# A feed-forward block in which GpSimd rounds the tokens and adds the outputs, and VectorE takes the statistics at the end of its turn

## The reference

```python
def bitlinear(x, W, b):
    w_scale = jnp.clip(jnp.mean(jnp.abs(W)), EPS, None)
    Wq = _ste(W, jnp.clip(jnp.round(W / w_scale), -1.0, 1.0) * w_scale)
    x_scale = jnp.clip(jnp.max(jnp.abs(x), axis=-1, keepdims=True), EPS, None)
    xq = _ste(x, jnp.clip(jnp.round(x * (QB / x_scale)), -QB - 1.0, QB) * (x_scale / QB))
    return jnp.einsum('bnd,hd->bnh', xq, Wq) + b
h = bitlinear(x, W1, b1)
h = jax.nn.gelu(h, approximate=False)
return bitlinear(h, W2, b2)
...
x = x + _L0_ffn_ref(_layernorm(x, axis=-1), L0_ffn_W1, L0_ffn_b1, L0_ffn_W2, L0_ffn_b2)
```

## Time and profile before

| | us |
|---|---|
| median of 3 runs | 934.14 (934.08 to 935.68) |
| span of the profiled execution, first to last instruction | 930.7 |
| own time of the profiled execution | not listed apart; the median lies 3.4 over the span |
| busy in the span: PE, DVE, ACT, POOL | 870.6, 631.0, 532.4, 388.8 |
| stretch 53.35 to 142.48, feed-forward turns: DVE, ACT, PE, POOL busy of 89.13 | 77.15, 68.14, 68.11, 41.87 |

### The profile page before, as it was taken

How to read it: one execution, slowest core, us unless ns; L and a number is a source line. 1 busy time by engine, 2 the same in 40 slices (tenths; PEclk the granted TensorE clock), 3 DMA queues, 4 the chain that set the end, 5 groups by cost and what they waited for, 6 DMA issues and landing times.

```text
span 930.7 us, 14992 instructions
## 1 busy us (share of the span) xinstructions
PE 870.6 (94%) x4295; PEld 611.3 (66%) x4300; DVE 631.0 (68%) x1274; ACT 532.4 (57%) x851; POOL 388.8 (42%) x334
## 2 busy tenths in 40 slices
PE   9977789889999999999999999999999999999992
PEld 4635455544555545555467787878888888888881
DVE  5788987856557557456388779856666666666666
ACT  2558885455675665765555534326666666666650
POOL 2144455434775746656505645612222222222210
PEclk9999999999999999999999999999999999999996
DMA  9500000019469578568564200078711288526405
GB/s 305 113 1 1 0 1 1 1 43 367 176 232 352 183 288 335 195 281 315 227 249 173 121 1 1 13 287 368 280 63 34 65 339 339 223 81 260 110 17 181
DMA packets 49909, 154.07 MB, mean 166 GB/s; under 512 B 6266, under 2 KB 24438, under 8 KB 44236
## 3 DMA queue, kind: packets, MB, share of 16 engines
q1 hardware_dynamic: 46124, 144.25, 41.3%
q0 software_dynamic: 3744, 9.31, 3.2%
HBM read 97.85 MB, written 56.62 MB: 166 GB/s over the span
## 4 chain that ended last, share of the span: by engine, by line
PE 68%; DVE 16%; ACT 6%; issue 4%; DMA 2%; POOL 2%; SPq 1%; DVEq 0%; ACTq 0%; POOLq 0%
PE banks L1043 12%; PE banks L1294 8%; PE banks L1296 8%; PE banks L1295 8%; PE banks L1012 4%; PE banks L1035 3%; PE banks L1036 3%; PE banks L1331 2%; PE banks L1333 2%; PE banks L1332 2%; PE banks L1307 2%; PE banks L950 2%; PE banks L916 1%; PE banks L999 1%; PE banks L1057 1%
## 5 line engine op out<-in xcount | busy, mean ns | idle before, releaser
L1043 PE MATMUL banks<-wexp 128*65 128x512 f32 (+1 forms) x288 | 148.1, 595 | 3.3 <-ACT wexp L1608 3.3
L674 POOL TENSOR_TENSOR cv_hl<-wexp,cv_hl 128x1024 fp32r<-128x1024 f32 x45 | 108.5, 2419 | 55.0 <-ACT cv_hl L1585 54.4
L1294 PE MATMUL banks<-ring,x_hi 128*128 x312 | 127.4, 408 | 0.0
L1296 PE MATMUL banks<-ring,x_lo 128*128 x312 | 122.1, 391 | 0.0
L1295 PE MATMUL banks<-ring,x_hi 128*128 x312 | 122.0, 391 | 0.0
L1608 ACT ACTIVATE wexp<-banks 128x512 f32<-128x512 f32 x128 | 76.5, 600 | 69.2 <-PE banks L1036 68.8
L2097 DVE TENSOR_REDUCE small<-banks 128x1 bf16<-128x1101 f32 x64 | 83.7, 1307 | 38.5 <-PE banks L1012 38.5
L1744 ACT ACTIVATE banks<-wexp 128x1024 f32 x72 | 73.5, 1020 | 47.7 <-DVE aux L2488 47.7
L1722 ACT ACTIVATE aux<-banks 128x512 f32<-128x512 f32 x78 | 46.7, 598 | 61.2 <-PE banks L1296 45.2
L1035 PE MATMUL banks<-q_hi,k_hl 128*128 128x512 f32 x144 | 74.3, 516 | 1.7 <-ACT q_lo L1576 1.0
L1296 PEld LDWEIGHTS banks<-ring,x_lo 128*128 128x128 f32 x312 | 58.6, 188 | 13.1
(11 more groups left out here) (373 smaller groups left out, 2186.6 us busy)
## 6 DMA issues: line engine op xcount, KB each, us to landing
wsplit<-cv_hl SPq DMA_DIRECT2D x45, 1024.0 KB, 8.0
ring<-wsplit SPq DMA_DIRECT2D x32, 1280.0 KB
wexp<-in_L_ffn_w SPq DMA_DIRECT2D x40, 512.0 KB, 5.9
wexp<-in_expert_biases SPq DMA_DIRECT2D x8, 1152.0 KB, 6.5
ring<-wsplit SPq DMA_DIRECT2D x4, 1024.0 KB, 8.3
wexp<-moe_y SPq DMA_DIRECT2D x7, 512.0 KB, 5.9
wexp<-in_L_ffn_sw SPq DMA_DIRECT2D x5, 512.0 KB, 10.2
x_sb<-in_x SPq DMA_DIRECT2D x4, 512.0 KB, 7.8
```

Source lines behind the costliest of these rows:

```text
L674: g.tensor_tensor(sides(hl[:, PIECE:2 * PIECE]), raw, sides(hl[:, 0:PIECE]).bitcast(f32), ALU.subtract).then_inc(s['cv_lo'], 1)
L1043: mm(pb[5 + half][0:DA, :], vh[b][0:w, c, :], pT[q % 3][0:w, :], start=c == 0, stop=c == len(KTILES) - 1).then_inc(s['a_pv'], 1)
L1294: mm(o[:], x_hi[u][:, kc, :], hi, start=kc == 0 and not primed, stop=False, skip_group_check=primed)
L1296: last = mm(o[:], x_lo[u][:, kc, :], hi, start=False, stop=primed and kc == KC - 1, skip_group_check=primed)
```

## The change

POOL's loop now also rounds the token before (`ffn_tokens(t - 1)`, after `f_by` has reached t) and adds an output (`ffn_result(t - 6)`). ACT copies the output out of the PSUM, times its step, into one of two buffers `y_part`, and rounds only token 15 itself. DVE loses `ffn_sum`; its statistics move to the end of the turn and wait for `f_res`, which POOL's addition raises. Rows are normalised as row times `rstd` plus `less_mean`, which one more DVE instruction per half makes. POOL's last six additions stand behind its roots and before its constants. A separate semaphore for the warm-up constant is dropped and its count added to another.

```diff
--- before.py
+++ after.py
@@ -190,6 +190,7 @@
...
         h_qT = [scr.take(HID, HC, bf16) for _ in range(2)]
+        y_part = [scr.take(D) for _ in range(2)]
         assert scr.at <= mark
...
@@ -270,6 +271,7 @@
...
         ln_r = sb("ln_r", [P, T])
+        less_mean = sb("less_mean", [P, T])
         gateT = sb("gateT", [P, KC, E])
...
@@ -605,16 +607,26 @@
...
             pool.wait_ge(s['g_xnT_full'], T // 4)
+            def ffn_tokens(t):
+                g.tensor_scalar(xn[:, t % 2, :], xn[:, t % 2, :], f_by[:, t % 2, 0:1], MAGIC, ALU.mult, ALU.add).then_inc(s['f_xm'], 1)
+
+            def ffn_result(t):
+                pool.wait_ge(s['f_yout'], t + 1)
+                g.tensor_tensor(x_sb[:, t, :], x_sb[:, t, :], y_part[t % 2], ALU.add).then_inc(s['f_res'], 1)
+
             for t in range(T):
...
                     pool.wait_ge(s['f_xqT_full'], t - 1)
-                g.tensor_scalar(xn[:, t % 2, :], x_sb[:, t, :], mv[:, t, 0:1], rstd[:, t:t + 1], ALU.subtract, ALU.mult).then_inc(s['f_xn'], 1)
+                g.tensor_scalar(xn[:, t % 2, :], x_sb[:, t, :], rstd[:, t:t + 1], less_mean[:, t:t + 1], ALU.mult, ALU.add).then_inc(s['f_xn'], 1)
+                if t >= 1:
+                    pool.wait_ge(s['f_by'], t)
+                    ffn_tokens(t - 1)
                 pool.wait_ge(s['f_xn'], t + 1)
-                if t >= 5:
-                    pool.wait_ge(s['f_by'], t)
                 g.tensor_tensor(x_sb[:, t, :], x_sb[:, t, :], b2_all[:], ALU.add).then_inc(s['f_pool'], 1)
+                if t >= 6:
+                    ffn_result(t - 6)
 
...
@@ -626,6 +638,8 @@
...
             pool.sem_inc(s['f_pool'], 1)
+            for t in range(T - 6, T):
+                ffn_result(t)
 
...
@@ -1510,14 +1524,23 @@
...
                 act.wait_ge(s['f_by'], i + 5)
-                if there(tokens):
+                if isinstance(tokens, int) and tokens == T - 1:
                     a(xn[:, u, :], xn[:, u, :], ACT.Copy, scale=f_by[:, u, 0:1], bias=MAGIC).then_inc(s['f_xm'], 1)
...
 
+            def ffn_sum(t, u):
+                act.wait_ge(s['f_y'], t + 1)
+                act.wait_ge(s['f_by'], t + 5)
+                if not isinstance(t, int) or t >= 2:
+                    act.wait_ge(s['f_res'], t - 1)
+                a(y_part[u], pb[6][:, 0:D], ACT.Copy, scale=f_step[:, 1 - u, 1:2]).then_inc(s['f_yout'], 1)
+
             def ffn_turn(i, u):
...
                     ffn_T(i + 3, 1 - u)
+                if there(i - 1):
+                    ffn_sum(i - 1, 1 - u)
                 if there(i):
...
@@ -1902,7 +1925,7 @@
...
                 norm(t0, t1, 0.0)
-                ve.sem_inc(s['f_rstd'], 1)
+                v.scalar_tensor_tensor(less_mean[:, t0:t1], mv[:, t0:t1, 0], -1.0, rstd[:, t0:t1], ALU.mult, ALU.mult).then_inc(s['f_rstd'], 1)
 
...
@@ -1975,29 +1998,24 @@
...
 
-            def ffn_sum(t, u):
-                ve.wait_ge(s['f_y'], t + 1)
-                ve.wait_ge(s['f_pool'], t + 1)
-                v.scalar_tensor_tensor(tile(t), pb[6][:, 0:D], f_step[:, 1 - u, 1:2], tile(t), ALU.mult, ALU.add)\
-                    .then_inc(s['f_yout'], 1)
-
             def ffn_statistics(t):
-                ve.wait_ge(s['f_yout'], t + 1)
-                statistics(t)
+                ve.wait_ge(s['f_res'], t + 1)
+                return statistics(t)
 
             def ffn_turn(i, u):
-                if there(i - 1):
-                    ffn_sum(i - 1, 1 - u)
                 if there(i + 1):
...
                     c = slice(0 if there(i + 3) else 1, 2 if there(i) else 1)
+                    if not isinstance(i, int) or i >= 2:
+                        ve.wait_ge(s['f_yout'], i - 1)
                     last = v.tensor_tensor(f_step[:, 1 - u, c], f_max[1 - u][:, c], wsc[:, c], ALU.mult)
-                    if not there(i + 1):
+                    if isinstance(i, int) and i < 0:
                         link(last)
-                if there(i - 1):
-                    ffn_statistics(i - 1)
+                    elif not there(i + 1):
+                        last.then_inc(s['f_by'], 1)
+                        ve.wait_ge(s['f_by'], i + 5)
                 if there(i + 4):
...
```

More of the change, by code:

```diff
@@ L327, in program @@
         eno, eno_sh = sb("eno", [P, 1]), sb("eno_sh", [P, 1])
-        names = """ld_x ld_l0 ld_ffn ld_l1 ld_route ld_w0 ld_w1 ld_w2 ld_bias1 w_ready cv_hi cv_lo const ld_x1 ld_x2 ld_x3 ld_w12 w_inv w_times warm prep_full prep_free ctx_n w_abs
+        names = """ld_x ld_l0 ld_ffn ld_l1 ld_route ld_w0 ld_w1 ld_w2 ld_bias1 w_ready cv_hi cv_lo const ld_x1 ld_x2 ld_x3 ld_w12 w_inv w_times prep_full prep_free ctx_n w_abs
             root_in root_out chain chain_pool
             g_xn g_xnT_full g_xnT g_sc g_sh g_p g_pT_full g_pT g_av
-            f_rstd f_xn f_by f_hm f_xm f_xqT_full f_xqT f_acc f_pre f_h f_amax f_hqT_full f_hqT f_y f_yout f_pool a_const a_q
+            f_rstd f_xn f_by f_hm f_xm f_xqT_full f_xqT f_acc f_pre f_h f_amax f_hqT_full f_hqT f_y f_yout f_res f_pool a_const a_q
             l_free l_xh l_xT_full l_xT l_qkv l_qk l_sq l_ss l_bo
@@ L579, in _ @@
             g.memset(ones[:], 1.0)
-            g.memset(ones_b[:], 1.0).then_inc(s['warm'], 1)
+            g.memset(ones_b[:], 1.0).then_inc(s['const'], 1)
             link(g.memset(ident[:], 0.0))
@@ L786, in warm @@
                     mm(pb[7][:], ones_b[:], ones_b[:].unsqueeze(1).to_broadcast([P, 4, P]), start=True, stop=True)
-            pe.wait_ge(s['warm'], 1)
+            pe.wait_ge(s['const'], 2)
             warm(28)
-            pe.wait_ge(s['const'], 2)
+            pe.wait_ge(s['const'], 3)
             pe.wait_ge(s['ld_l0'], NLD['ld_l0'])
@@ L1443, in kept @@
                 last.then_inc(s['prep_free'], 1)
-            act.wait_ge(s['const'], 2)
+            act.wait_ge(s['const'], 3)
             ready(ACT.Sqrt)
@@ L1803, in norm @@
                 link(v.reciprocal(d, t_))
-            ve.wait_ge(s['const'], 2)
+            ve.wait_ge(s['const'], 3)
             link(v.tensor_scalar(eno_i[:], eno_i[:], 31, None, ALU.bitwise_and))
@@ L2010, in ffn_turn @@
                     ffn_hidden(i + 2, u)
+                if there(i - 1):
+                    last = ffn_statistics(i - 1)
+                    if isinstance(i, int) and i in (T - 8, T):
+                        link(last)
             ss_l = p0[:].rearrange("p a b -> p (a b)")
```

## The result

The changed kernel takes **940.82 us** (median of 4 runs, 940.55 to 942.64) against 934.14: 6.7 us more, ratio 1.0069, 95% interval 1.0055 to 1.0084. Forecast were 946.0 in a range of 940 to 954. So the time lies inside the range, but 5.1 under the forecast and only 0.8 above its low end. The profiled execution took 940.55 itself, with a span of 938.8 (930.7 before): the spans lie 8.1 apart, the medians 6.7.

A forecast was written before the change was run, and what follows sets the result against it. With no engine full, a ring of waits was taken to set the pace, 4.33 us a turn. Head -0.9, turns +2.4 and +2.1, tail +8.0 made +11.6 on 934.14: forecast 946, range 940 to 954.

The forecast's parts named there:

- The ring through POOL: Feed-forward turns: each DVE reciprocal leads through POOL's rounding and additions to the next, 4.59 us a turn instead of 4.33.
- c: Price of POOL's tensor_scalar with product and addition over 256 columns: taken as 0.55 us, range 0.39 to 1.22.
- 0.11 for the address: Extra per turn in the loop's six turns, for the statistics' address made after the wait; an estimate, 0 to 0.2.
- rival 1: POOL's scalar forms stay at 1.22 us, ten laps cost 0.67 more each: 953; chance 0.18.
- Turns 1 to 8: Seven feed-forward turns from reciprocal to reciprocal: 32.8 us against 30.3, +2.4.
- The head: Start of the stage: first reciprocal of turn 1 earlier by 0.9 us (bounds 0 and 1.34).
- Turns 8 to 12: Turns with the aggregation of eight rows and POOL's roots: 19.4 us against 17.3, +2.1.
- d: How late PE is from turn 12 on: -0.9 + 2.4 + 2.1 = 3.6 us.
- The tail: End of the block: POOL's constants stand behind output 15, delaying the fourth sum of squares, +8 us beyond d.
- 2: Rival: the shared port takes more of DVE, up to 0.6 us in each of nine turns: 951; chance 0.14.
- 3: Rival: the ring does not close through POOL, turns fall to ACT's ring of 4.06 us: 938; chance 0.10.
- 4: Rival: faster, as 3, with the constants and first squares hidden as well: 930; chance 0.04.

The follow-up runs named there:

- add_first: The changed kernel with POOL's addition of output t-6 moved ahead of the rounding that waits for f_by: 937.42 us.
- const_early: The changed kernel with POOL's constants moved ahead of its last four additions: 940.40 us.
- all_three: The changed kernel with POOL's queue reordered: additions ahead of roundings, one between root steps, constants ahead of the last four additions, two squares earlier: 932.14 us.
- keep_clock: The changed kernel with 22 matmuls on ones put into PE's idle 5.38 us ahead of the transposes of token 6: 946.02 us.
- old_form: The changed kernel with rows normalised by subtraction and product again, the less_mean instruction kept: 943.40 us.
- const_again: const_early measured once more, on one chip with a repetition of the changed kernel (941.76 us): 942.81 us.
- const_clock: const_early plus 6 matmuls on ones ahead of the transposes of token 6 and 10 ahead of those of token 8: 940.44 us.
- round_only: The kernel before with only the token rounding and the new normalisation form moved to POOL; DVE still adds the outputs: 930.22 us.
- round_only_old: The kernel before with POOL's rounding alone, rows still normalised by subtraction and product: 930.42 us.

## Why the prediction was right, and where its sizes were not

**The ring through POOL: right.** It closes exactly as laid out (chain of waits above), and add_first takes it away. Its pieces from 99.11: 0.27 to the rounding (0.32 forecast), 0.43 to the bias addition (c, 0.55), 0.69 (0.71), 0.91 to the statistics (0.77, and 0.11 for the address), then 0.34, 0.06 (0.12), 0.33, 1.25 and 0.20: 4.48 against 4.70. **c** was 0.473 as a duration and 0.43 from start to start, near the lower bound; so the nearest row by form, L613's 1.22, was the wrong one to fear, and rival 1 fell. The 0.11 for the address had no row behind it; the runs give 0.14, since the statistics start 0.91 behind POOL's addition in the loop and 0.77 in turn 11, which is written out (124.15 to 124.92). Turns 1 to 8: +1.84 for a forecast +2.4.

**The head: mis-sized.** -2.0 instead of -0.9 (75.91 against 77.92), beyond the bound of 1.34. I counted DVE's wait for the output alone. Its addition (0.48) and its statistics (0.43) also left the place ahead of turn 1's largest values, and turn 1's reciprocal then waited for ACT alone, 0.60 at 74.44.

**Turns 8 to 12.** +1.37 instead of +2.1: 5.36 for the turn with the aggregation (5.5), 4.32 for the next (4.6), 9.01 for the two through the roots (9.3). The wait behind the roots is there: 1.46 at 124.92. So d was 1.2, not 3.6; of the 2.4 that were missing 1.1 lie in the head.

**The tail: right in place and size.** From turn 12 to the fourth sum the loss is 8.8 - 1.2 = 7.6 for a forecast 8. It is not one cost, though: const_early removes 3.2 of it, and the rest of the queue's order, changed in all_three, the remainder.

**From the fourth sum to the end** I carried the sum on unchanged. It was 8.8 there, 7.8 at the ninth sum and at `q_lo`, 7.0 at 877, 8.1 at the end of the spans (DVE's last additions waited 0.95 for their transfers instead of 0.16), and 6.7 in the medians. The last step, 1.4, is no change in what the kernel does: I added the 3.4 by which the median before lay over its profiled span, and behind the changed kernel's span the median lies 2.0. The first step, 1.0, comes from DVE's scales: from the fourth sum to the normalisation of token 8 they and what stands around them took 6.57 before (147.20 to 153.77) and 4.98 in the changed kernel, where they mostly missed POOL's squares while PE ran at its low clock. I had written that the low clock has slack until token 8. By the trace it hadn't quite: DVE's normalisation of token 8 ran from 160.97 to 161.91, and PE took it at 162.43. But keep_clock shows that this did not cost the time it seemed to.

**The rivals.** 1 fell with c. 2's mechanism didn't show in the turns of the changed kernel (its factors take 0.15 to 0.18 in all), but does in all_three; its size there is 0.27 a turn. 3 is what add_first makes: 4.10 a turn (forecast 4.06) and 937.42 (938), by a ring that goes through PE's second product too. 4 is nearly all_three. Forecast +11.6, measured +6.7: 1.1 head, 0.6 and 0.7 the two stretches of turns, 0.4 tail, and 2.1 behind it. All five made the forecast too high: the places of gain and loss were right, their sizes were not, and the time just stayed in the range.

## What to carry to other kernels

When work goes to an engine with time to spare, write down its queue in order and ask of every entry who waits for it, and whether what stands ahead of it depends on that same waiter. Here POOL worked 17.23 of 32.16 us, and two orders of the same instructions lie almost 9 us apart. Work that nobody waits for yet belongs ahead of the last item that arrives late, not behind it. A microsecond saved in front of a short idle time of PE need not arrive at the end: read several landmarks of the trace, not the span alone, before you credit or blame an edit.

## What the runs showed of the hardware

**A tensor_scalar on POOL has no one price per width.** Over 256 columns of f32, product and addition took 0.473 us with one operand of the scalar pair read from memory and 0.555 with both; subtraction and product took 1.222, also with both. Whether the subtraction or where `mv` lies costs it wasn't separated. The Trainium skill (GPSIMD Engine Reference, section 3.1) has one rate for all bodies of up to two operations; the forecast's estimate from that rate, 0.4, lies 0.07 and 0.15 under the first two durations; the third is three times as long, so the one rate does not hold for it.

**Small DVE instructions beside a POOL instruction** often took 0.42 to 1.01 instead of 0.17 to 0.2, until POOL's ended (all_three, keep_clock), or 0.17 when they started together with it (add_first, 100.77). A turn can lock in either way for as long as it repeats. The long ones agree with the Trainium skill (SBUF — State Buffer, "Who interferes with whom"), by which, where DVE and GpSimd both want the shared ports, the one that issues first keeps them for its whole instruction. Not all were held, though: in the kernel before, the first instruction of the factors took 0.17 at 81.90, beside a POOL normalisation that ran from 81.14 to 82.36, and 0.42 at 86.22 beside the next. What decides this isn't shown.

**TensorE's clock after idle time.** Eight matmuls took 2.75 at full clock, 4.37 to 4.97 behind 5.38 to 5.40 of idle time (the changed kernel, add_first, old_form; granted clock 0.50 from 156 to 158 in the changed kernel, the lower of the two levels), 4.13 to 4.28 behind 2.53 (const_early, const_again, keep_clock), and again 2.75 behind 1.48 (const_early, 151.16). A second fall before `q_lo` cost 1.7 to 2.6 in seven of the twelve executions of the table, though PE's bursts and idle times just ahead of it were alike; it shows in DVE's idle time ahead of `q_lo`, 2.85 to 2.87 without and 4.51 to 5.46 with it. The same two matmuls took 1.97 in keep_clock and 1.07 in the changed kernel:

```profile
208.15 1.97 PE L1061 MATMUL banks<-wexp 128*65 128x512 f32 x2 [1.21 <-ACT wexp L1635]
```

```profile
206.20 1.07 PE L1057 MATMUL banks<-wexp 128*65 128x512 f32 x2 [1.20 <-ACT wexp L1631]
```

It fell in const_early, const_again, const_clock, keep_clock, old_form, all_three and round_only, but not in the changed kernel, its repetition, add_first, round_only_old, or the profiled execution of before. Why there and not here stays open. It probably also spreads the times, though only the profiled executions show where the clock fell: the runs of the kernel before on one chip went from 932.84 at a mean clock of 0.990 to 939.32 at 0.982.
